# Graph attention with a layer norm: ELU by ScalarE and two adding DMAs, means by VectorE, both ends reordered

## The reference

```
h     = x @ W                      (per head, 32 columns)
th    = tanh(h);  s = th . w_src;  d = th . w_dst      (per head)
e[n,m]= leaky_relu(s[n] + d[m], 0.2), masked by adj[n,m]
att   = softmax(e) @ h + b
elu   = att if att > 0 else exp(att) - 1
gate  = sigmoid(x @ H_w.T + H_b)
out   = layernorm(x + gate * elu + (1 - gate) * x)     (over the 384 features, no scale or shift)
```

## Time and profile before

| | us |
|---|---|
| median of 3 runs | 671.02 (670.91 to 671.18) |
| the profiled execution's own time | 670.99 |
| its span (first to last instruction) | 668.9 |
| busy: PE / DVE / POOL / ACT | 646.2 / 646.5 / 565.1 / 447.7 |
| mean granted TensorE clock | 0.994 |
| DMA moved | 117.6 MB, 176 GB/s over the span |
| adding DMAs (POOL's queue) | 30 of 768 KB, 18.8% of the DMA engines' span |

### The profile page before, as it was taken

The page is one execution under the profiler, slowest core; times in us unless marked ns, Lnnn a source line. Parts: engine busy times, 40 slices in busy tenths (PEclk is TensorE's granted clock), DMA queues, the critical chain, the costliest instruction groups (busy, mean ns, idle before and its releaser), DMA issues.

```text
span 668.9 us, 12479 instructions
## 1 busy us (share of the span) xinstructions
PE 646.2 (97%) x3279; PEld 366.9 (55%) x3279; DVE 646.5 (97%) x1171; ACT 447.7 (67%) x936; POOL 565.1 (84%) x444
## 2 busy tenths in 40 slices
PE   8999999999999999999999999999999999998982
PEld 5554656555565555555555555565656556564530
DVE  7999999999999999999999999999999999999796
ACT  5524558587675867767586775858677585966754
POOL 2536898989989998998989999899989989896482
PEclk9999999999999999999999999999999999999997
DMA  6336558568485766847586585857758485765502
GB/s 205 117 100 196 174 128 235 159 168 243 146 239 139 224 169 164 228 157 233 145 214 180 147 240 144 234 136 202 216 145 227 136 244 140 205 179 146 202 31 95
DMA packets 54715, 117.62 MB, mean 176 GB/s; under 512 B 7074, under 2 KB 32420, under 8 KB 54692
## 3 DMA queue, kind: packets, MB, share of 16 engines
q1 hardware_dynamic: 42180, 81.56, 37.7%
q0 software_dynamic: 4320, 23.59, 18.8%
q10 hardware_dynamic: 8192, 12.19, 5.4%
HBM read 104.35 MB, written 12.98 MB: 175 GB/s over the span
## 4 chain that ended last, share of the span: by engine, by line
PE 80%; ACT 9%; DVE 5%; issue 3%; DMA 1%; POOL 1%; ACTq 0%; SPq 0%; POOLq 0%; DVEq 0%
PE out_T L1022 43%; PE hg L930 30%; PE tr L1030 6%; ACT xT_hi L460 3%; ACT scratch L550 3%; DVE ew L789 2%; ACT att_T L522 2%; DVE sd L751 1%; DMA xT_in<-in_xT 1%; DVE th_w L736 1%; PE hg L960 1%; PE hg L964 0%; ACT scratch L557 0%; POOL th_w L296 0%; DVE hb_sum L725 0%
## 5 line engine op out<-in xcount | busy, mean ns | idle before, releaser
L789 DVE SCALAR_TENSOR_TENSOR ew<-v_all,u,adj 128x512 f32<-128x512 f32 x768 | 524.8, 727 | 1.9 <-DMA v_all<-v_rows 0.9
L1022 PE MATMUL out_T<-ew,vals 128*64 128x512 f32 x1536 | 356.4, 599 | 0.0
L1022 PEld LDWEIGHTS out_T<-ew,vals 128*64 128x64 f32 x1536 | 105.2, 136 | 186.9 <-issue 146.7
L296 POOL TENSOR_TENSOR th_w<-th,score_w 128x768 f32<-128x768 f32 x58 | 127.9, 2206 | 23.4 <-DVE th_w L736 10.2
L522 ACT ACTIVATE att_T<-out_T,out_bias 128x512 f32<-128x512 f32 x96 | 66.1, 689 | 105.1 <-PE out_T L1022 104.7
L930 PE MATMUL hg<-w_hi,xT_hi 128*128 128x384 f32 x384 | 99.5, 367 | 2.7 <-ACT xT_hi L460 1.5
L930 PEld LDWEIGHTS hg<-w_hi,xT_hi 128*128 128x128 f32 x384 | 61.7, 191 | 52.8 <-issue 50.7
L930 PE MATMUL hg<-w_lo,xT_hi 128*128 128x384 f32 x384 | 88.6, 338 | 0.0
L930 PE MATMUL hg<-w_hi,xT_lo 128*128 128x384 f32 x384 | 87.7, 335 | 0.0
L930 PEld LDWEIGHTS hg<-w_lo,xT_hi 128*128 128x128 f32 x384 | 69.5, 188 | 0.0
L930 PEld LDWEIGHTS hg<-w_hi,xT_lo 128*128 128x128 f32 x384 | 68.9, 188 | 0.0
(11 more groups left out here) (116 smaller groups left out, 681.4 us busy)
## 6 DMA issues: line engine op xcount, KB each, us to landing
v_all<-v_rows SPq DMA_DIRECT2D x95, 512.0 KB, 4.7
xT_in<-in_xT SPq DMA_DIRECT2D x16, 768.0 KB, 9.3
h_sb<-in_bias POOLq DMA_DIRECT2D x15, 768.0 KB, 6.6
x_in<-in_x SPq DMA_DIRECT2D x15, 768.0 KB, 4.6
gate_tanh<-in_H_b POOLq DMA_DIRECT2D x15, 768.0 KB, 9.5
out<-y ACTq DMA_DIRECT2D x15, 768.0 KB, 3.8
adj_in<-in_adjT SPq DMA_DIRECT2D x16, 256.0 KB, 9.5
v_rows<-v_turn SPq DMA_DIRECT2D x64, 6.0 KB
```

What stands on the lines that cost most here:

```text
L296: g.tensor_tensor(th_w[:, c % 2], th[:, c].unsqueeze(1).broadcast_to([P, 2, D]), score_w[:], ALU.mult).then_inc(S["thw_done"], 1)
L789: ve.scalar_tensor_tensor(out=ew[:, (2 * C * j + i) % SLOTS, :], in0=v_all[:, j % VSLOTS, k], scalar=u[:, q, c, h:h + 1], in1=ADJ[c][:], o ...
L1022: te.matmul(OUT[VW * k:VW * k + VW, :], vals[:, q, c, h, :], ew[:, t % SLOTS, :], start=(c == 0), stop=(c == C - 1)).then_inc(S["ew_free"], 1)
```

## The change

ELU of a steady batch is taken apart. x_forms makes -x - 1 instead of x + 1, at the end of the step before. ScalarE makes Relu(att - 1) (above, into ex), Relu(1 - att) (below, in place in att) and Exp of minus that (in place). POOL issues two adding DMAs from SBUF to SBUF: ex is added to x_minus (the tile x_plus1), then att. The result is max(a, 0) + exp(min(a, 0)) - 1 - x = elu - x, where a = att - 1. VectorE's `elu` and POOL's subtraction are left only for batch 14, which the last step finishes in the old way. The means: VectorE turns hb_tot in 32x32 blocks and sums each block's rows, at the start of pair 5, and one matmul with a mask `mean_sel` of TINY / N takes the place of six; two activations copy it out in place of four. POOL builds the mask at the start. In batch 0 POOL weighs all four chunks. In the last step gates 0 come ahead of the transposes on PE, `gates_last(1)` ahead of pair 1's copy and the last gate pass ahead of pair 2's on ScalarE, the quotient of pair 1 stands two edges later, MIDDLE and FINAL get their own sums and statistics, and the last store is cut in four.

```diff
-                m = out_bias[:, q].rearrange("p (i s) -> p i s", s=2)
-                for r in range(4):
-                    rows = slice(VW * (r % 2), VW * (r % 2) + E)
-                    means = mean_first_ps if isinstance(b, int) and b == 0 else mean_ps
-                    a.activation(m[rows, :, r // 2], means[E * r:E * r + E, :], ACT.Copy).then_inc(S["out_bias_done"], 1)
+                m = mean_ps.rearrange("p (j k) -> p k j", k=2)
+                for k in range(2):
+                    rows = slice(VW * k, VW * k + E)
+                    a.activation(out_bias[rows, q], m[rows, k], ACT.Copy).then_inc(S["out_bias_done"], 2)
...
+            def add_above(b):
+                pool.dma_start(x_minus, ex[:].rearrange("p c d -> p (c d)"), accum_op=ALU.add).then_inc(S["add_rel"], 16)
+            def add_below(b, q):
+                pool.dma_start(x_minus, att[:, q].rearrange("p c d -> p (c d)"), accum_op=ALU.add).then_inc(S["add_exp"], 16)
+            def mix(b):
+                pool.wait_ge(S["gate1_done"], b + 1)
+                pool.wait_ge(S["add_exp"], 16 * b + 16)
+                g.tensor_tensor(x_plus1[:], gate[:], x_plus1[:], ALU.mult).then_inc(S["mixed"], 2)
...
             # weigh: waits ahead of the half-sum of chunk 0 and of chunk 2
+                if c == 0 and not first:
+                    pool.wait_ge(S["rel_done"], b - 1)
+                    pool.wait_ge(S["x_forms_done"], b - 1)
+                if c == 2 and not first:
+                    pool.wait_ge(S["elu_exp_done"], b - 1)
+                    pool.wait_ge(S["add_rel"], 16 * b - 16)
...
             # POOL's step
-                    for c in range(2 if first else 0, C):
-                        weigh(b + 1, c)
+                    for c in range(C):
+                        weigh(b + 1, c, first)
+                        if c == 0 and not first:
+                            add_above(b - 1)
+                        if c == 2 and not first:
+                            add_below(b - 1, 1 - q)
...
             # ScalarE
-                a.activation(x_plus1[:], x_in[:], ACT.Identity, bias=plus1[:, 0:1]).then_inc(S["x_forms_done"], 1)
+                a.activation(x_plus1[:], x_in[:], ACT.Identity, bias=minus1[:, 0:1], scale=-1.0).then_inc(S["x_forms_done"], 1)
+            def elu_above(b, q):
+                act.wait_ge(S["att_done"], HP * b + HP)
+                if not isinstance(b, int) or b:
+                    act.wait_ge(S["add_rel"], 16 * b)
+                a.activation(ex[:], att[:, q], ACT.Relu, bias=minus1[:, 0:1]).then_inc(S["rel_done"], 1)
+            def elu_below(b, q):
+                a.activation(att[:, q], att[:, q], ACT.Relu, bias=plus1[:, 0:1], scale=-1.0).then_inc(S["neg_done"], 1)
+            def elu_below_exp(b, q):
+                act.wait_ge(S["neg_done"], b + 1)
+                a.activation(att[:, q], att[:, q], ACT.Exp, scale=-1.0).then_inc(S["elu_exp_done"], 1)
...
-                    elu_exp(b - 1, 1 - q)
+                    elu_above(b - 1, 1 - q)
                 features(b + 1, 1)
-                if not isinstance(b, int) or b > 1:
-                    normalise(b - 2, 0, 2)
                 if not first:
+                    elu_below(b - 1, 1 - q)
                     copy_out(b, q, 0)
+                    elu_below_exp(b - 1, 1 - q)
                 features(b + 1, 2)
                 if not isinstance(b, int) or b > 1:
-                    normalise(b - 2, 2, C)
+                    normalise(b - 2)
                 features(b + 1, 3)
-                if not first:
-                    x_forms(b - 1)
...
                 copy_out(b, q, 5)
+                x_forms(b)
...
             # VectorE
+            def mean_parts(b, q):
+                dve.wait_ge(S["hb_sum_done"], 2 * b)
+                ve.transpose(hb_turn, hb_tot[:, q]).then_inc(S["hb_turned"], 1)
+                dve.wait_ge(S["hb_turned"], b)
...
+                ve.tensor_reduce(mean_part[:], hb_turn.rearrange("p (h k) -> p h k", k=VB), AX.X, ALU.add).then_inc(S["part_done"], 1)
...
-                    if j == 1 and not first:
+                    if j == 1 and last:
                         between[1] = [lambda: elu(b - 1, 1 - q)]
...
+                    if j == 5 and not last:
+                        between[0] = [lambda: mean_parts(b + 1, 1 - q)]
                     if j:
-                        at = (None, 6, 5, 7, 7, 6)[j]
+                        at = (None, 6, 7 if last else 5, 7, 7, 6)[j]
...
             # the last batch on VectorE
                 elu_late(0, MIDDLE)
+                gated(MIDDLE, 1)
                 dve.wait_ge(S["y_early_done"], 2)
+                with_rest(MIDDLE, 1)
                 statistics(0, EARLY)
                 inverses()
                 quotients()
-                gated(MIDDLE, 1)
+                dve.wait_ge(S["y_late_done"], 2)
+                statistics(1, MIDDLE)
                 elu_late(1, FINAL)
                 gated(FINAL, 2)
...
             # TensorE
-                for i in range(H // 4):
-                    last = te.matmul(mean_ps[:, i:i + 1], hb_tot[:, q, i * P:(i + 1) * P], mean_w[:, 0:1],
-                                     start=True, stop=True)
-                last.then_inc(S["hm_done"], 1)
+                te.matmul(mean_ps, mean_sel[:], mean_part[:], start=True, stop=True).then_inc(S["hm_done"], 1)
...
-                transpose_out(b - 1, HP - 1)
                 gates(b, q, 0, True)
+                transpose_out(b - 1, HP - 1)
```

More of the change, by code:

```diff
@@ L114, in gat_layernorm @@
         squares = sb("squares", [P, C])
[L115 removed]
+        stats = sb("stats", [P, C, 3, 6])
         mv = sb("mv", [P, C, 2])
@@ L252, in after @@
             def after():
[L253 to L256, removed]
+                for c in range(2, C):
+                    sp.wait_ge(S["last_y_done"], c - 1)
+                    sp.dma_start(out_v[B - 1][:, c], y_last[:, c]).then_inc(S["st_last"], 16)
+                sp.wait_ge(S["st_y"], 16 * B + 32)
+                sp.wait_ge(S["st_last"], 32)
             program(sp, step, before, after)
@@ L286, in before, with weigh @@
                     split_low(1, 1, c)
-                pool.wait_ge(S["gate_bias_split"], 2)
-                g.tensor_tensor(gate_bias[:], gate_bias_in, gate_bias_off, ALU.subtract).then_inc(S["gate_bias_done"], 1)
-            def weigh(b, c):
+            def weigh(b, c, first):
                 pool.wait_ge(S["th_done"], C * b + c + 1)
[L292 to L295, removed]
+                pool.wait_ge(S["sd_done"], C * b + c - 1)
                 g.tensor_tensor(th_w[:, c % 2], th[:, c].unsqueeze(1).broadcast_to([P, 2, D]), score_w[:],
@@ L366, in step_last @@
             def step_last(b, q):
-                subtract_x(b - 1)
-                mix(b - 1)
+                mix_before_last(b - 1)
                 pool.wait_ge(S["gate1_done"], B)
@@ L507, in out_biases @@
                     act.wait_ge(S["outT_copied"], HP * (b - 1))
-                m = out_bias[:, q].rearrange("p (i s) -> p i s", s=2)
-                for r in range(4):
-                    rows = slice(VW * (r % 2), VW * (r % 2) + E)
-                    means = mean_first_ps if isinstance(b, int) and b == 0 else mean_ps
-                    a.activation(m[rows, :, r // 2], means[E * r:E * r + E, :], ACT.Copy).then_inc(S["out_bias_done"], 1)
+                if isinstance(b, int) and b == 0:
+                    m = out_bias[:, q].rearrange("p (i s) -> p i s", s=2)
+                    for i in range(4):
+                        rows = slice(VW * (i % 2), VW * (i % 2) + E)
+                        a.activation(m[rows, :, i // 2], mean_first_ps[E * i:E * i + E, :], ACT.Copy).then_inc(S["out_bias_done"], 1)
+                    return
+                m = mean_ps.rearrange("p (j k) -> p k j", k=2)
+                for k in range(2):
+                    rows = slice(VW * k, VW * k + E)
+                    a.activation(out_bias[rows, q], m[rows, k], ACT.Copy).then_inc(S["out_bias_done"], 2)
             def copy_out(b, q, j):
@@ L744, in head_sums @@
             def head_sums(b, c):
-                if isinstance(b, int) and (b == 0 or b == 1 and c < 2):
+                if isinstance(b, int) and b == 0:
                     dve.wait_ge(S["thw_done"], C * b + c + 1)
@@ L800, in quotients @@
                 def quotients():
+                    if not isinstance(b, int) or b > 1:
+                        dve.wait_ge(S["add_exp"], 16 * b - 16)
                     dve.wait_ge(S["inv_done"], HP * b + j + 1)
@@ L1035, in step_last @@
             def step_last(b, q):
+                gates(b, q, 0, True)
                 transpose_out(b - 1, HP - 1)
-                gates(b, q, 0, True)
                 attend(b, q, 0)
```

77 lines of the change are left out of this document (50 added, 27 removed).

## The result

The changed kernel takes 692.97 us (691.24 to 695.43), the kernel before in the same rounds 671.01: a ratio of 1.033, with a 95% interval of 1.030 to 1.036. It is slower by 3.3%. The profiled execution took 693.4 us with a span of 691.5, at a clock of 0.994 as before, so the clock explains nothing.

What follows compares the result with a forecast made beforehand. TensorE was taken to bound the steady batches, VectorE about 0.4 us behind. 670.99 - 1.5 (start) - 3.2 (end) + 9.1 (fourteen batches at +0.65) = 675.4, stated as 675 us; range 664 to 692.

Steps and rivals of the forecast that it cites:

- I take the upper part of the h_sb row, 7.0 to 7.3: Landing time in us assumed for the ELU's adding DMAs, from 768 KB adds into h_sb that took 6.1 to 7.3.
- The bound: First ELU add must land within 6.95 us of issue for pair 5's edge 7; each us later costs one a batch.
- the adds come late: Rival, chance 0.20: first ELU add takes 8.0 to 9.5 us like the gate's; time 681 to 700, range 679 to 705.
- Late by 0.7 to 0.95 us instead of 0.6: Pair 5's edge 7: lateness raised by add landings of 7.0 to 7.3 us; +0.75 us a batch entered the sum.
- The place, edge 7 of pair 5: Tightest meeting of VectorE and TensorE, VectorE early by 0.25 us; the new wait of each batch was expected there.
- The means on VectorE: Transpose and sum at the start of pair 5 cost 1.05 us (0.75 to 1.4), making edge 7 0.6 us late.
- The rival of the hidden means: Rival, chance 0.35: edge 7 of pair 5 stays in time and only the ends count; 665 us, range 663 to 669.6.
- The removed matmuls and copies: Six small matmuls fewer on TensorE worth 0; two copies fewer on ScalarE worth 0.1 us a batch, 1.4 over fourteen.
- Three passes on ScalarE: ELU's one pass becomes three, +3.2 us on an engine with 11 us free; cost 0, with 0.3 us to spare.
- ELU off VectorE: Removing the 1.91 us instruction leaves VectorE only 0.18 us earlier after the maximum over the keys.
- The start: Batch 0: POOL takes 2.6 us of work off VectorE, pair 3 starts near 50.0 instead of 51.91; -1.5 us.
- The end: Last batch: reordered gates, later quotient, smaller final columns and stores shorten waits of TensorE and VectorE; -3.2 us.

Runs made afterwards that it cites:

- e4: Changed kernel with both adding DMAs of the ELU moving one of four chunks, three quarters of the ELU left out: 675.64 us, ratio 1.007.
- e5: Changed kernel with only the first ELU add cut to a quarter of its bytes, the second whole: 676.16 us, ratio 1.008.
- e7: Changed kernel with the adding DMA of the gate bias cut to a quarter, ELU adds whole: 676.83 us, ratio 1.009.
- e1: Changed kernel with the old means (six matmuls, four copies, nothing on VectorE); adds and reordered ends stay: 689.87 us, ratio 1.030.
- e3: Changed kernel with only the two reordered ends; steady ELU and means as before: 664.56 us, ratio 0.990 to the kernel before.
- e9: Changed kernel, whole computation, with the gate bias's adding DMA issued 2.9 us earlier: 680.50 us, ratio 1.014.
- e10: Changed kernel with the gate bias's adding DMA issued 2.9 us earlier and the old means, nothing left out: 670.87 us, ratio 1.000.
- e2: Changed kernel with the old steady ELU, no SBUF-to-SBUF adds; means on VectorE and both reordered ends stay: 674.60 us, ratio 1.005.
- e8: Changed kernel with the old means and both ELU adds cut to a quarter, three quarters of the ELU left out: 665.27 us, ratio 0.992.

## Why the prediction was wrong

**The step that failed: "I take the upper part of the h_sb row, 7.0 to 7.3".** The first add took 8.7 us in the median, from 6.4 to 10.3; e4, e5 and e7 show that its landing is the cost. The other row, the gate add's 9.5, was the one in the same traffic, and the earlier trace rows spoke for it. The prediction set it aside because "the h_sb adds got their 6.6 with other loads issued beside them". The queues of the kernel before say otherwise: the stretch from 319 to 325, with an h_sb add issued at 318.64, then the first microseconds of a gate add issued at 301.48, from 302 to 305.

```profile
q0 software_dynamic: 141, 0.79, 76.7%
q1 hardware_dynamic: 37, 0.13, 5.4%
...
q1 hardware_dynamic: 139, 0.52, 66.7%
q0 software_dynamic: 7, 0.04, 7.1%
```

Beside the h_sb add SyncE's queue had 5% of the engines' time, beside the gate add's start 67%. Issued loads are not moving loads.

**The bound was right.** Landing within 6.95 us of the issue is what keeps edge 7 on time with the means in the way, and 8.00 without them; each us later was to cost a us a batch. With the mean landings in it this gives 1.83 us late in the changed kernel and 1.53 in e1; the batches are 1.81 and 1.66 us longer than e3's. In e9 (7.63) and e10 (7.79) it gives 0.68 and nothing against 1.02 and 0.33 measured, so it is short by 0.3 there. The two batches with 6.4 and 7.3 us took no more than e2's, because the means make the edge 0.8 us late in any case. Put into the prediction's own sum, 8.78 gives 670.99 - 4.7 + 14 x (1.83 - 0.1) = 690.5, and the 3.0 us that the end did not give (below) make it 693.5, less 0.4 that the start gave beyond the forecast; the profiled execution took 693.4. This was worked out afterwards, with the landing that was missing before. The rival "the adds come late" has the mechanism and nearly the price: 681 us for 8.0 and 700 for 9.5 lie around 693 at 8.7. It had a chance of 0.20, and the stated range, 664 to 692, left its upper part out.

**"Late by 0.7 to 0.95 us instead of 0.6": a slip in the sum.** By the bound, 7.0 to 7.3 us is 0.05 to 0.35 late with the means already counted, less than the 0.6 of the other path. The sum should then have kept 0.6, 14 x 0.5 = 7.0, and come to 673.3; it added the two.

**The Trainium skill's fit** (DMA: Bandwidth & Descriptors, Anatomy of one DMA), 3.8 us as an estimate for 768 KB, is far from these adds: the shortest of 28 took 5.8 us, and the first adds of e4, 192 KB, still took 4.0 to 5.2. The measurement decides.

**The place, edge 7 of pair 5: right in the main.** Pair 5 is where every batch is stretched. That an add of 9.6 us or more holds up pair 2 as well, whose edges stand behind the head sum on VectorE, the prediction did not see.

**The means on VectorE: the two instructions right, their cost right by luck.** Transpose 0.56 and sum 0.55 us, 1.05 with the hand-over, all as estimated. Pair 5's attend takes 4.48 us for 3.65, 0.83 more, in e2, where VectorE keeps its ELU, and in e4, where it does not. So the slack of 0.25 us held (1.05 - 0.25 = 0.80), and the 0.18 us that the ELU's removal was to give did not come. The sum's 0.75 - 0.1 = 0.65 us a batch meets the 0.66 of e2 against e3 only because 0.15 us for the adds stood in it, in place of that 0.18. The rival of the hidden means (665 us) falls: e3 and e8 reach 665 only without them.

**The removed matmuls and copies: right.** In e2 the transposes of pair 4 start 0.96 us after the means' matmul, with a wait of 0.57 us for the copy, so the shorter matmul gained nothing. From the end of pair 5's attend to the next one, e2 takes 3.73 us in the mean and e3 3.91: the copies are worth 0.18 us a batch, for 0.1 predicted.

**Three passes on ScalarE: right.** 1.0 us in e4 against e2, 0.7 in e8 against e3, over a whole run. A thing that I missed: with late edges in pair 5, ScalarE's adjacency copies wait for the slots of VectorE (16.4 us in 28 times, before nearly nothing), and what stands behind them shifts.

**ELU off VectorE:** it gave PE nothing, not even the 0.18 us. VectorE's busy time fell by 12 us, and e4, which has this relief without the slow adds, is at e2's 39.93 us.

**The start: -1.5 predicted, -1.9 measured.** **The end: -3.2 predicted.** Alone the edit gives -3.8 (e3), in the changed kernel -0.2. The last gate add took 10.9 us, ScalarE's tanh pass waited 0.37 us for it, and pair 0's transposes waited for the copy behind:

```profile
647.16 1.49 ACT L572 ACTIVATE gate_tanh<-gate_tanh 128x1536 f32<-128x1536 f32 x1 [0.37 <-DMA gate_tanh<-in_H_b]
...
650.88 0.66 PE L1097 MATMUL tr<-ident,att_T 128*128 128x128 f32 x4 [1.39 <-ACT att_T L560]
```

Of the 3.6 us that are missing against e3, 1.7 are batch 14's own pair 5 (5.32 us for 3.65; e2, with the means alone, has 4.53), 1.2 lie between the starts of pair 0 and pair 1 of the last batch (10.0 us for 8.8), where this wait is, and 0.7 come after the start of the last pair 5 (17.1 us for 16.4), nearly all of it behind VectorE's last instruction; e4 has these 0.7 too, and their cause was not sought. The intended gain was there: VectorE's wait of 3.63 us is 0.95.

The forecast of 675 is near e2 (674.6) and e4 (675.6), the change with its adds left out or short. The 17.3 us between e4 and the changed kernel are what was missing.

## What to carry to other kernels

A DMA that is to hide behind work has to be sized by transfers that run in the same part of the batch, behind the same neighbours, and not by the same kind of transfer elsewhere; where two such rows differ by 3 us, and what waits for the transfer has 7 us, the slower row is the forecast until something speaks against it. Look for which DMA moves just ahead of the critical one: moving that one by 2.9 us was worth 12.5 us here. And before work is shifted to the engine just below the bound, compare its idle time in a batch (0.5 us here) with what it is given (1.05): the difference is of the size of what was paid in every batch (0.66). A part's price read by taking it out holds only if the other transfers land as before: e1's 3 us would have hidden a price of 10. The version to keep is the two ends alone, 1% under the kernel before.

## What the runs showed of the hardware

An adding DMA within SBUF of 768 KB moved at about 0.22 MB a us with the 16 engines full, where the loads before it moved 0.38 MB a us in the same share of time. The Trainium skill (DMA: Bandwidth & Descriptors, SWDGE vs HWDGE vs iDMA) says that a DMA engine takes turns between its internal queues. Over stretches of some us the trace shows something coarser: first 106% of the time for q1 with nothing for q0, though the add had been issued, then 105% for q0; and in another batch 82% for the gate add beside 13% for the loads. About half of those three us is the start that any add has; the rest is a delay behind SyncE's packets.

The second adds of e1 are the steadiest case: 13 of the 14 landed in 5.8 us, 1.5 to the first packet, 4.0 from the first packet's start to the last one's, and 0.4 from the last packet's end to the semaphore. A first add that took 10 us spent 4.2 before its first packet and 5.2 to 5.8 on its packets (changed kernel and e1).

Quartering the bytes of both adds took 4 us off the first one's landing (8.7 to 4.6 us) and 1 us off the second's (6.2 to 5.2).
